# Stage three of a gated cross-attention kernel: router products turned to wide ones, filling products ahead, the slot list read first, gates turned among the shared products

## The reference

```python
logits = xt @ router_w + router_b
scores = jax.nn.softmax(logits, axis=-1) + router_bias
g = scores.reshape(T, GROUPS, E // GROUPS)
_, gidx = jax.lax.top_k(g.max(axis=-1), LIM)
...
_, idx = jax.lax.top_k(masked, K)
...
h = jax.nn.silu(xt @ w1 + b1) * (xt @ w2 + b2)
...
```

## Time and profile before

| what | value |
|---|---|
| time, median of 3 runs | 1595.41 us (1594.83 to 1595.83) |
| the profiled execution's own time | 1598.46 us |
| its span | 1596.6 us |
| mean granted clock of TensorE | 0.966 |
| TensorE busy | 1498.1 us, 94% |
| VectorE busy | 986.8 us, 62% |
| ScalarE busy | 770.2 us, 48% |
| GpSimd busy | 165.9 us, 10% |

### The profile page before, as it was taken

The page is one execution under the profiler, slowest core; times in us unless marked ns, Lnnn a source line. Parts: engine busy times, 40 slices in busy tenths (PEclk is TensorE's granted clock), DMA queues, the critical chain, the costliest instruction groups (busy, mean ns, idle before and its releaser), DMA issues. The chain is left out here.

```text
span 1596.6 us, 26398 instructions
## 1 busy us (share of the span) xinstructions
PE 1498.1 (94%) x9200; PEld 1337.7 (84%) x9200; DVE 986.8 (62%) x1650; ACT 770.2 (48%) x2010; POOL 165.9 (10%) x162
## 2 busy tenths in 40 slices
PE   6999968999999999999999999999997897899997
PEld 5888868999999999899999889999995786788875
DVE  4322237666777666577766666766665477666648
ACT  3111226555556555465555555655553222677750
POOL 0000000000000000000000000000000502577750
PEclk9999989999999999999999999999999678999999
DMA  6556452111232111222211221221100403578437
GB/s 225 163 167 170 135 195 93 53 67 39 86 106 74 47 47 66 67 73 75 92 40 47 76 91 67 73 68 46 46 8 1 149 1 100 187 254 269 162 97 281
DMA packets 97515, 163.75 MB, mean 103 GB/s; under 512 B 12469, under 2 KB 47321, under 8 KB 93326
## 3 DMA queue, kind: packets, MB, share of 16 engines
q1 hardware_dynamic: 87438, 145.69, 27.6%
q0 software_dynamic: 9984, 16.82, 3.4%
HBM read 128.36 MB, written 49.81 MB: 112 GB/s over the span
## 5 line engine op out<-in xcount | busy, mean ns | idle before, releaser
L84 PE MATMUL ps_q<-xt,wq_hi 128*128 128x256 f32 x1024 | 302.6, 296 | 11.2 <-DMA xt<-x_scratch 11.2
L86 PE MATMUL ps_q<-xt,wq_hi 128*128 128x256 f32 x1024 | 291.9, 285 | 0.0
L85 PE MATMUL ps_q<-xt,wq_lo 128*128 128x256 f32 x1024 | 291.8, 285 | 0.0
L656 ACT ACTIVATE s_sb<-s_sb,nmax 128x128 f32<-128x128 f32 x512 | 199.6, 391 | 129.8 <-DVE nmax L734 129.8
L732 DVE TENSOR_TENSOR s_sb<-ps_s,s_cross 128x512 f32<-128x512 f32 x128 | 88.6, 692 | 242.0 <-ACT s_cross L645 242.0
L645 ACT ACTIVATE s_cross<-ps_s 128x512 f32<-128x512 f32 x128 | 76.4, 597 | 279.3 <-PE ps_s L809 279.3
L84 PEld LDWEIGHTS ps_q<-xt,wq_hi 128*128 128x128 f32 x1024 | 198.8, 194 | 11.9 <-DMA xt<-x_scratch 11.6
L84 PE MATMUL ps_y<-wo_hi,o_hi 128*128 128x512 f32 x512 | 203.0, 396 | 0.9 <-DVE y L712 0.9
L85 PE MATMUL ps_y<-wo_hi,o_lo 128*128 128x512 f32 x512 | 203.3, 397 | 0.0
L86 PE MATMUL ps_y<-wo_lo,o_hi 128*128 128x512 f32 x512 | 203.2, 397 | 0.0
L85 PEld LDWEIGHTS ps_q<-xt,wq_lo 128*128 128x128 f32 x1024 | 199.1, 194 | 0.0
(11 more groups left out here) (244 smaller groups left out, 3305.5 us busy)
## 6 DMA issues: line engine op xcount, KB each, us to landing
xt<-x_scratch SPq DMA_DIRECT2D x32, 1024.0 KB, 4.8
w_raw<-in_L_ffn_ew SPq DMA_DIRECT2D x93, 256.0 KB, 3.4
v_full<-v_out SPq DMA_DIRECT2D x64, 128.0 KB, 2.6
k_full<-k_out SPq DMA_DIRECT2D x16, 512.0 KB, 2.8
w_raw<-in_L_xattn_Wq SPq DMA_DIRECT2D x16, 512.0 KB, 4.1
kt_raw<-k_full SPq DMA_DIRECT2D x32, 256.0 KB, 2.6
vt_raw<-v_full SPq DMA_DIRECT2D x32, 256.0 KB, 2.6
w_raw<-in_L_xattn_Wo SPq DMA_DIRECT2D x16, 512.0 KB, 4.3
```

Of the source, the lines that this page charges most:

```text
L84: pe.matmul(out, w_hi, x_hi, start=first, stop=False)
L85: pe.matmul(out, w_lo, x_hi, start=False, stop=False)
L86: return pe.matmul(out, w_hi, x_lo, start=False, stop=last)
L656: last = act.activation(s_sb[:, i], s_sb[:, i], ACT.Exp, bias=nmax[:, i:i + 1], accum_out=sums[:, i:i + 1])
```

## The change

It has five parts, all in stage three.

1. TensorE starts with 14 products of ones by ones (`WARM`), 512 columns each, whose result nobody reads, ahead of the first transposes. The small transpose of `shared_rows` moves behind tile 3.
2. The logits of a whole octet come from eight products in which `rw` stands as weights and 512 tokens move through (`octet_logits`), into 32 rows; ScalarE copies these (`copy_logits`) and four small products per octet with the constant `fold` add the hi and lo parts and turn them back (`turn_logits`). VectorE has one addition of logits for two.
3. Loads and splits are reordered: SP loads the first half's weights first, the second half's at tile 6, b3 in two transfers in place of six; the splits move to later tiles; GpSimd makes `fold` between tiles 3 and 5.
4. The gates are multiplied right after the choice, transposed by TensorE among `pe_up(2)`, `pe_up(3)` and the hot products, copied three times by ScalarE, and `gates_low` is GpSimd's, from SBUF copies. Slots 0 and 1 have no gate work. The bias product moves from the second shared half to the first.
5. VectorE finishes only the first octet's h and reads the slot list, then works out the slots' experts. TensorE's down products of octet 0 come ahead of the slot biases. The first half uses three banks for four.

`gates_low` is in GpSimd's list, `copy_logits` and `gates_high` in ScalarE's, `octet_logits` in TensorE's.

```diff
-            if o:
-                pe.wait_ge(self.y_added, 4 * o - 4 + i + 1)
+            n, banks = 4 * o + i, len(self.ps_down)
+            if n >= banks:
+                pe.wait_ge(self.y_added, n - banks + 1)
...
             if extra is not None:
                 stacked, b3 = extra
-                last = pe.matmul(self.ps_down[i][:], stacked[:, 512 * o + P * i:512 * o + P * i + P], b3[:],
+                last = pe.matmul(bank[:], stacked[:, 512 * o + P * i:512 * o + P * i + P], b3[:],
                                  start=False, stop=True)
...
-    CONSTS = 20
+    CONSTS = 22
+    WARM = 14
...
-        shared = [SharedHalf(b, half, work, weights[half], banks[0:4], [banks[i] for i in (6, 7, 4, 5)], y, moe)
+        shared = [SharedHalf(b, half, work, weights[half], banks[0:4], [banks[6], banks[7], banks[4], banks[5]][:4 if half else 3], y, moe)
...
+            def gates_low(i):
+                pool.wait_ge(gates_hi_made, i + 1)
+                pool.wait_ge(gates_copied, i + 1)
+                tokens = slice(512 * i, 512 * i + 512)
+                pool.tensor_tensor(stacked[32:64, tokens], gates_t[i % 2], f32(stacked[0:32, tokens]),
+                                   ALU.subtract).then_inc(gates_lo_made, 1)
...
+            def copy_logits(o):
+                act.wait_ge(logits_t_done, o + 1)
+                if o >= 2:
+                    act.wait_ge(logits_turned, o - 1)
+                act.activation(logits_t[o % 2], ps_l[0:2 * E, :], ACT.Copy).then_inc(logits_t_copied, 1)
...
+            def gates_high(i):
+                act.wait_ge(gates_turned, i + 1)
+                tokens = slice(512 * i, 512 * i + 512)
+                act.activation(stacked[0:32, tokens], ps_g[i % 2][0:32, :], ACT.Copy)
+                act.activation(stacked[64:96, tokens], ps_g[i % 2][0:32, :], ACT.Copy).then_inc(gates_hi_made, 1)
+                if i >= 2:
+                    act.wait_ge(gates_lo_made, i - 1)
+                act.activation(gates_t[i % 2], ps_g[i % 2][0:32, :], ACT.Copy).then_inc(gates_copied, 1)
...
+            def octet_logits(o):
+                pe.wait_ge(x_lo_made, 4 * o + 4)
...
+                for c in range(C):
+                    pe.matmul(ps_l[0:2 * E, :], rw[:, c].rearrange("p s e -> p (s e)"), x_hi[:, c, tokens],
+                              start=c == 0, stop=False)
+                    last = pe.matmul(ps_l[0:E, :], rw[:, c, 0], x_lo[:, c, tokens], start=False, stop=c == C - 1)
+                last.then_inc(logits_t_done, 1)
...
+            for i in range(WARM):
+                pe.matmul(ps_warm[:], ones_r[:], ones_r[:].unsqueeze(1).to_broadcast([P, 4, P]), start=True, stop=True)
...
+            pe.wait_ge(b3_lo_made, 1)
+            pe.wait_ge(gates_lo_made, 4)
+            pe.wait_ge(slots_made, 3)
+            shared[0].pe_down(pe, 0, (stacked, b3))
...
-                if isinstance(s, int) and s < 2:
-                    pe.wait_ge(gates_made, 1)
-                    pe.wait_ge(shared[0].y_added, TILES)
-                    turn_gates(2 * s)
-                    turn_gates(2 * s + 1)
-                    if s == 1:
-                        pe.wait_ge(gates_lo_made, 4)
```

More of the change, by code:

```diff
@@ L1135, in stage_three @@
             earlier_r = e.sb("earlier_r", [P, P], F32R)
-            b3_raw = e.sb("b3_raw", [3 * 32, D])
+            b3_raw = work[0][0][0:32]
+            logits_t = [work[1][i][0:2 * E] for i in range(2)]
+            gates_t = [rows_in[1][0:2 * E, i] for i in range(2)]
+            fold = e.sb("fold", [2 * E, E])
             probs = logits
@@ L1153, in stage_three @@
         xs_lo = [b.sb(f"xs_lo{i}", [P, C, SLOT], F32R) for i in range(2)]
[L1154 to L1157, removed]
+        w_parts = [[b.sb(f"w3_{part}{i}", [P, 3, 512], F32R) for part in ("hi", "lo")] for i in range(2)]
+        w_hi, w_lo = zip(*w_parts)
         silu, h_sb, h_hi, h_lo = [[buf[:, 0:SLOT] for buf in pair] for pair in work]
@@ L1371, in scatter @@
                         bounds_check=2 * T - 1, oob_is_err=False).then_inc(y_scattered[s % 2], 16)
-            pool.wait_ge(consts_made, CONSTS)
+            for i in range(4):
+                gates_low(i)
+            pool.wait_ge(gates_lo_made, 4)
+            pool.memset(rows_in[1][:], 0.0).then_inc(consts_made, 1)
+            pool.wait_ge(consts_made, CONSTS + 1)
             for r in range(RING):
@@ L1414, in _ @@
                 shared[0].act_gate(act, o)
+            for i in range(4):
+                gates_high(i)
             for o in range(2):
@@ L1643, in _ @@
                             ps_bias[:, 0:2 * ROOM]).then_inc(bias_copied, 1)
-            dve.wait_ge(mask_made, 1)
-            dve.tensor_tensor(gates[:, :, 0:E], scores[:], f32(mask[:, 0:TILES]), ALU.mult).then_inc(gates_made, 1)
-            def gates_low(i):
-                dve.wait_ge(gates_hi_made, i + 1)
-                tokens = slice(512 * i, 512 * i + 512)
-                dve.tensor_tensor(stacked[32:64, tokens], ps_g[i % 2][0:32, :], f32(stacked[0:32, tokens]),
-                                  ALU.subtract).then_inc(gates_lo_made, 1)
-            shared[0].dve_add(dve, 0, gain)
             shared[0].dve_h(dve, 2)
@@ L1690, in slot @@
                     w_down_low(s + 1, 1 - r)
-                if isinstance(s, int) and s < 2:
-                    gates_low(2 * s)
-                    gates_low(2 * s + 1)
             w_up_low(0, 0)
@@ L1763, in turn_gates @@
                 if i >= 2:
[L1764 removed]
+                    pe.wait_ge(gates_copied, i - 1)
                 for n in range(4 * i, 4 * i + 4):
@@ L1784, in _ @@
             last.then_inc(slot_bias_done, 1)
-            pe.wait_ge(slots_made, 3)
-            pe.wait_ge(bias_copied, 2)
-            for o in range(3):
-                shared[0].pe_down(pe, o)
+            shared[0].pe_down(pe, 1, (stacked, b3))
+            shared[0].pe_down(pe, 2, (stacked, b3))
             def turn(s, r):
```

192 lines of the change are left out of this document (111 added, 81 removed).

## The result

The changed kernel took 1583.47 us (median of 4, 1579.57 to 1584.44), the kernel before beside it 1595.62 (median of 4, 1594.83 to 1597.9): ratio 0.9924, 95% interval 0.991 to 0.9939. It is faster by 12.15 us, or 0.8%, where 19.4 (1595.41 to 1576) were forecast; 1583.47 lies just inside the range that ends at 1584.

The account below looks back on a forecast made before the run. TensorE at half clock was taken to bound the router part, VectorE the kernel's end. Terms of −9.9, −0.4, +1.7, −3.7, +1.4, −9.0 and 0 summed to −19.9 us, giving 1576 us, range 1568 to 1584.

Parts of the forecast that it names:

- gates turned early: Between mask and hot products: sixteen gate transposes on TensorE lie on the path, +1.7 us.
- list first: Between VectorE's last hot column and TensorE's first down product: reading the slot list earlier shortens 7.1 us to 3.4, −3.7.
- down products: First half's down products: four products per tile, three banks, VectorE sets the pace, some clock loss; +1.4 us (0.3 to 2.2).
- behind slot 3: The tail, with the second half and reordered loads: loads stay hidden and nothing changes, 0 us.
- Router: Router part up to the logits: wide products and fillers replace narrow products, clock partly at half; −9.9 us.
- rival one: Router: fillers start before the clock falls and wide products keep it; −25.2 us in all, 1570; chance 0.17.
- To the mask: Routing chain from logits to mask: VectorE has one operation on the logits fewer; −0.4 us.
- Against 1329.4 both are hidden: Before the first down product: gates_low on GpSimd, reckoned to end at 1325.2 or 1323.2, finishes before TensorE's start at 1329.4.
- Rival three: Before the down products: gates_low is slow on GpSimd, held off by VectorE; 3 to 5 us late, 1580; chance 0.06.
- Next late is the hot product itself, which nothing here moves: At the slot list: after the reordering the hot products, out at 1328.1, are next late and unmoved by the change.
- Slots 0 to 2: Early slots: without gate work they run at the loop's pace, 17.95 us against 26.97; −9.0 us.
- rival five: Slot loop: weight loads pace it in another phase against gathers and scatters; slower, 1601 at 6.9 us per slot; chance 0.02.

Follow-up runs that it names:

- first trace: First profiled execution of the changed kernel, nothing further edited: 1579.57 us, stage three 335.86 us.
- the repeat: The changed kernel again on chip B, nothing edited: ratio 0.9906 to the kernel before.
- hot fillers: The changed kernel with 8 more fillers behind the second hot batch and 4 behind the third: 4.2 us from last hot column to first down product.

## Why the prediction was right or wrong

The direction and the range held; the size was 1.6 times too large. Up to slot 3 the mechanism of each term is there in the traces. Two were mis-sized in both traces (the gates turned early, the list first), the down products in the first trace alone, and the part behind slot 3, put at 0, wasn't 0. By its own steps, from T0:

- **Router, −9.9.** The first trace has −11.9, the repeat and five others −8.7 to −9.0. So the sum is 0.9 to 1.2 us off for the usual execution. Its tiles ahead of the first wide block end at T0 + 9.5 (1255.8), but the block starts at 11.0 and 11.2 in the two traces, and TensorE's last waits there are for VectorE's `x_lo`, not for GpSimd. That one execution may keep the clock and gain 3 us more was rival one; it hid 2 us of the later misses in the first trace, which is luck.
- **To the mask, −0.4.** −0.5.
- **Gates turned early, +1.7.** +3.65 from the mask to the last hot column; with gates_low off GpSimd or turned to writes +1.75 (23.1 against 21.4). The sixteen transposes were priced right. The step that failed is "Against 1329.4 both are hidden": I asked only whether gates_low would be late, and it wasn't, done at 1307.9. I didn't ask whom it slows. Rival three had the right mechanism with the wrong victim: VectorE was held off, not GpSimd.
- **List first, −3.7.** −1.9 in the first trace, −3.0 in the repeat, −3.6 with hot fillers. The order does what was reckoned; the clock, lost in the longer wait, took the rest. The failed sentence is "Next late is the hot product itself, which nothing here moves": it was moved by 1.9 and slowed from 2.05 to 3.78.
- **Down products, +1.4.** From the first to the transposes ahead of slot 0's products 23.4 in the first trace (+3.1), 21.8 in the repeat (+1.5). In the repeat the forecast held to 0.1 us. The first trace began these products at half clock, carried in from the step before (0.77 at 1318.17; 0.47 in the repeat), and was 1.4 us later at tile 11. The 1.1 us for the clock in this term was an estimate with no row for its size; in both traces the clock did fall behind the wait of 2.88 ahead of tile 11. VectorE set the pace only for the most part: without the fourth products this part is 1.4 us shorter than in the first trace.
- **Slots 0 to 2, −9.0.** 1359.82 − 1341.53 = 18.3 against 26.97: −8.7.
- **Behind slot 3, 0.** +1.8 in the first trace. On chip C it is 216.5 from slot 3's low part to the end in the kernel before and 217.3 to 217.4 in three changed ones, so about 1 us is lasting. In the first trace all of it lies in the 27 slots (162.78 us against 161.05). TensorE waits 6.0 us in all for gathered rows there, against 3.4 before, and on chip C 5.6 to 5.7 against 3.9; ScalarE waits 4.4 for weights against 2.8. So the slots' transfers come later against their users, which looks like rival five's mechanism at a small size. No run moves the transfers, so the cause stays open.

Up to slot 3 that is −16.2 in the first trace, −15.5 in the repeat, for −19.9; with 1 us behind it, some −14.5. The measured gains are 12.15 (9.7 to 14.4) and, on chip B, 15.1 (12.7 to 17.6), on either side of it. The step from the profiled execution to the median (3.05 off) did no harm in itself, but it shows the trap: stage three took 350.28 in that execution and 350.74 in another, while T0 moved by 5.6 us between traces, so its surplus probably lay ahead of T0, where the change can't reach.

## What to carry to other kernels

When work is moved to an engine with time to spare, ask not only whether it ends in time but what its SBUF reads do to the engine beside it: a hidden operation can still slow the one that isn't. Fillers ahead of a stretch buy little if what follows doesn't hold the clock (0.4 to 0.7 us here); two in each gap and six in the last held it through the router and brought the logits to 33.7 in both executions seen, 0.3 past the first trace's 33.4. Compare traces from the start of the changed stage, and take a second trace of the same kernel before a clock's behaviour is put down to the change.

## What the runs showed of the hardware

- A 32 x 512 subtraction on GpSimd with both inputs in SBUF took 1.26 to 2.16 us and made each VectorE operation that started while it ran, with both inputs in SBUF, 0.8 to 1.1 us longer; a memset of the same size took 0.52 and cost VectorE nothing. The Trainium skill, "SBUF — State Buffer", "Who interferes with whom", says that a VectorE instruction with two SBUF inputs contends with a GpSimd one that reads SBUF, not with one that only writes; the rows agree on both halves.
- In the kernel before with 14 fillers, TensorE's clock fell from full to half at 1255.3, at a wait of 1.13 us among transposes and products of 16 and 32 columns, and was still at half when the logits came at 1283.9, though TensorE was busy 20.00 of 20 us from 1260 to 1280.
- The slots took 5.97 to 6.03 us each in the first traces and on chip C, 6.31 to 6.60 on chips A and B, with the same instructions. On A and B, and only there, ScalarE stood 17.5 to 25.5 us in all ahead of `s_silu`, with no releaser in the profile.
